# Message-passing network, two layers: where the transposes of the new rows lie in PSUM, and the order of the sums

## Chip, cores, metric

One core of a Trainium2 chip. The metric is the device time of one execution in microseconds, the median of the runs; lower is better. All times below are microseconds unless marked ns.

## What is computed

Two graph layers over 50,000 nodes of 160 values (64 scalars and 32 vectors of 3) and 50,000 edges sorted by `dst`. In both, a small network of the edge's features gives 192 weights for each edge, the source's row is multiplied by them and by the edge's four harmonics, the messages are summed by `dst`, and a linear map goes over the sums.

```python
h = jnp.maximum(_layernorm(x, axis=-1), 0.0)
x = x + _L0_gnn_ref(h, edge_attr_4, edge_attr_8, ...)        # layer 1
h = jnp.maximum(_layernorm(x, axis=-1), 0.0)
x = x + _L1_gnn_ref(h, node_vec1, src, dst, edge_attr_4, edge_attr_10, ...)   # layer 2

# in _L0_gnn_ref
xs, xv = s @ W1_s / np.sqrt(MUL0), jnp.einsum('nmc,mk->nkc', v, W1_v) / np.sqrt(MUL1)
w = jax.nn.silu(edge_embed @ fc_w1 + fc_b1) @ fc_w2 + fc_b2
msg = jnp.concatenate([m0_a, m0_b, m1_a..., m1_b...], axis=1)   # w * xs[src], xv[src] * sh
agg = jax.ops.segment_sum(msg, dst, num_segments=n) / np.sqrt(AVG_DEG)
out = agg @ W2 + node_features @ Wsc      # gates: silu(out_s), vectors times gates
return node_features + feats
```

## The kernel before

`one_layer` is called twice, with `first` true for layer 1. Everything that follows is about layer 1 unless it says otherwise. The work is cut into NB = 205 turns (41 steps of 5 pairs); a turn `t` has two tiles of 128 edges and two of 128 nodes. Each engine runs a `step` for s = 0, 1, ..., in which `T(k)` is the turn s-k: the stages of one turn are spread over nine steps. Within an engine the order of the stages is the order of the calls in `step`, written out by hand; between engines there are semaphores. `eng.wait_ge(sem, n)` holds the engine's queue until sem is n, `hold` does the same and leaves it out for counts of 0 or less. A stage adds 1 to its semaphore when its last instruction is done, so `wait_ge(xw_done, t.n + 1)` waits for the stage of turn t.n itself.

TensorE's step: sums of tile 0 of T(4) (L1607), radial product of T(2) (L1567), sums of tile 1 of T(4) (L1607), outputs of T(5) (L1622, L1629), `pre` of T(8) (L1651, the next layer's products of the new rows), edges of T(2) (L1583, L1586, L1590), `transposes2` of T(7) (L1639, the new rows after norm and relu, `h2`), `transposes` of T(1) (L1553, L1556).

ScalarE's step: feature casts for layer 2 in some turns (L544), `copy_hT2` of T(8) (L1475), `copy_hT` of T(2) (L1413), `copy_agg` of T(4) (L1449), the hidden activation of T(2) (L1395), `node_h2` of T(7) (L1466), `node_h` of T(1) (L1404, the `hn` pair), `scale_pre` of T(8) (L1483), `gates` of T(5) (L1458), the issue of the DMA that stores `base_tab` (L1511, behind a wait for `scale_pre`'s end), and `copy_xw` of T(2) (L1422 and, scaled by a harmonic, two of L1429), whose end is `scaled_ready`. The next radial product waits for it.

PSUM has eight banks of 512 float32 columns. Before, `front_ps` takes four: the transposes for `hT` fill columns 0 to 767 of its flattened width (bank 0 and half of bank 1), `hT2_ps` columns 768 to 1151 (the other half of bank 1 and the first 128 columns of bank 2), and `xw_ps` is banks 2 and 3, with the edges' products from column 128 of each and the radial product in the first 128 of bank 3. `agg_ps` and `out_ps` have two banks each; `agg_ps` holds 384 columns of each bank, one bank for each tile.

An engine may not read a bank while TensorE writes into it, so the code waits by bank. Bank 2 is shared by a third of `hT2_ps` and the products that `copy_xw` reads; hence two waits that the change takes out:

```python
hold(act, hT2_done, t.n - 4)                                            # copy_xw, t = T(2)
pe.wait_ge(scaled_ready, t.n + 1 if t.serial else min(t.n + 5, NB))     # transposes2, t = T(7)
```

With t = T(2) the first is for the transposes of T(7) of the same step.

After the loop a serial pass handles nodes with very many edges, then layer 2 runs with the same code and fewer stages.

Of the kernel before, what the change touches and what calls it, by code (L numbers as in the profile page):

```python
# [33 lines left out]
P = 128  # L34
# [7 lines left out]
NT = P  # L42
# [96 lines left out]
def build(nc, x, node_col, edge_rec, dst_rows, dst_next, row_last, dst_flat, ee, wts, out):  # L139
# [10 lines left out]
    with ExitStack() as ctx:  # L150
# [85 lines left out]
        front_ps = ps("front_ps", [P, 2 * PAIR, 512])  # L236
        agg_ps = ps("agg_ps", [P, PAIR, 512])
# [523 lines left out]
def one_layer(nc, ctx, layer, node_rows, edge_rows, new_dram, v):  # L761
# [9 lines left out]
    front_ps, agg_ps, out_ps = v["front_ps"], v["agg_ps"], v["out_ps"]  # L771
    hT_ps, xw_ps = front_ps[:, 0:PAIR, :], front_ps[:, PAIR:2 * PAIR, :]
    front = front_ps[:, :, :].rearrange("p b c -> p (b c)")
# [7 lines left out]
    both_ps, hT2_ps = front[:, 0:HE + HN], front[:, HE + HN:HE + 2 * HN]  # L781

    if first:
        hid_ps = xw_ps[:, 1, 0:P]
        w_ps = xw_ps[:, :, P:P + xw]
    else:
        hid_ps = xw_ps[:, 1, 0:PAIR * P].rearrange("p (j e) -> p j e", j=PAIR)
        w_ps = xw_ps[:, 0, 0:PAIR * WN].rearrange("p (j c) -> p j c", j=PAIR)
# [129 lines left out]
    with nc.Block() as block:  # L918
# [470 lines left out]
        def _(act):  # L1389
# [18 lines left out]
            def copy_hT(t):  # L1408
                b = t.tiles
                act.wait_ge(hT_done, t.n + 1)  # L1410
                hold(act, out_done, t.freed_m(RING))
                hold(act, xw_done, t.freed(RING))
                act.activation(hT[:, t.slot, :], both_ps, ACT.Relu).then_inc(hT_copied, 1)  # L1413

            def copy_xw(t):
                b = t.tiles
                act.wait_ge(xw_done, t.n + 1)
                hold(act, msg_ready, t.freed(2))
                if first:
                    if not t.serial:  # L1420
                        hold(act, hT2_done, t.n - 4)
                    act.copy(xw_sb[:, t.half, 0:b, 0:D + W_SS], w_ps[:, 0:b, 0:D + W_SS]).then_inc(xw_copied, 1)  # L1422
                    act.wait_ge(she_ready, t.n + 1)
                else:
                    act.copy(xw_sb[:, t.half, 0:b, D:D + W_SS], w_ps[:, 0:b, 0:W_SS]).then_inc(xw_copied, 1)
                    if t.serial:
                        act.wait_ge(win_in[t.slot], window_loads(t))
                for j in range(b):
                    ins = act.activation(xw_sb[:, t.half, j, D + W_SS:D + WN], w_ps[:, j, xw - SW:xw] if first else w_ps[:, j, W_SS:WN],  # L1429
                                         ACT.Copy, scale=harmonics(t)[:, j, 0:1])  # L1430
                ins.then_inc(scaled_ready, 1)
# [38 lines left out]
            def copy_hT2(t):  # L1470
                b = t.tiles
                act.wait_ge(hT2_done, t.m + 1)
                wait_hT(act, hT_done, t, PRE - 2)
                hold(act, pre_done, t.freed_m(1))
                act.copy(hT2[:, :], hT2_ps).then_inc(hT2_copied, 1)  # L1475
# [63 lines left out]
        def _(pe):  # L1539
# [9 lines left out]
            def transposes(t):  # L1549
                hold(pe, hT_copied, t.freed(1))  # L1550
                pe.wait_ge(he_ready, t.n + 1)
                for c in range(PARTS_X):
                    pe.transpose(front[:, c * P:(c + 1) * P], pair_cols(he[:, t.half, c, :, :]), ident[:, :])  # L1553
                pe.wait_ge(hn_ready, t.n + 1)
                for c in (2, 0, 1):
                    ins = pe.transpose(front[:, node_cols(c):node_cols(c) + NT], pair_cols(hn[0:NT, t.half, c, :, :]), ident[0:NT, 0:NT])  # L1556
# [38 lines left out]
            def sums(t, tiles):  # L1595

                flat = msg[:, :, :, :, :].rearrange("p h j c m -> p h j (c m)")
                if tiles[0] == 0:
# [10 lines left out]
                if tiles[-1] == t.tiles - 1:  # L1609
# [23 lines left out]
            def transposes2(t):  # L1633
# [3 lines left out]
                pe.wait_ge(scaled_ready, t.n + 1 if t.serial else min(t.n + 5, NB))  # L1637
                for c in range(PARTS_X):
                    ins = pe.transpose(hT2_ps[:, c * NT:(c + 1) * NT], pair_cols(h2[:, c, :, :]), ident[0:NT, 0:NT])  # L1639
# [17 lines left out]
            def step(T):  # L1657
                if t := T(4):
                    sums(t, [0] if first else [0, 1])
                if (t := T(2)) and first:  # L1660
                    radial(t)
                if (t := T(4)) and first:
                    sums(t, [1])
# [127 lines left out]
```

## Time and profile before

| | |
|---|---|
| median of 3 runs | 2412.83 (2403.69 to 2425.43) |
| the profiled execution, its own time | 2389.98 |
| its span, first to last instruction | 2388.2 |
| TensorE matmul busy | 2176.7 (91%) |
| TensorE weight loads busy | 2045.3 (86%) |
| VectorE busy | 1909.6 (80%) |
| ScalarE busy | 1930.8 (81%) |
| GpSimd busy | 1541.1 (65%) |
| mean granted TensorE clock | 0.968 of full |

The trace names instructions by the line of the kernel and groups them; `PEld` is a weight load of TensorE, `ACTq` an instruction of ScalarE's queue that issues a DMA. Busy shares are means over the whole program; layer 1's loop is the first three fifths of it. The ends of matmuls are modelled.

### The profile page before, as it was taken

To read this page: it belongs to the slowest core of one execution; us is meant where nothing else is said; L and a number is where in the kernel's file an instruction comes from. 1 tells how busy PE (TensorE), PEld (TensorE's weight loads), DVE (VectorE), ACT (ScalarE), POOL (GpSimd) and SP (SyncE) were. 2 spreads that over 40 slices of the span, in tenths; PEclk is the share of its full clock that TensorE was granted. 3 is DMA by queue.
4 is the path that set the end of the run, shared out by engine and by line. 5 is a ranking of instruction groups with operands and counts; after the bars stand their busy time and mean duration, and the time that the engine had idled before them with its cause. 6 is when DMAs were issued, how large, how long until landed. Compare 5 with 4: busy or idle time off the path is not lost. (4 is left out here: it accounts for less than half of the span.)

```text
span 2388.2 us, 79221 instructions
## 1 busy us (share of the span) xinstructions
PE 2176.7 (91%) x22003; PEld 2045.3 (86%) x22004; DVE 1909.6 (80%) x8636; ACT 1930.8 (81%) x5167; POOL 1541.1 (65%) x1925
## 2 busy tenths in 40 slices
PE   0889999999999999999999999559999999999997
PEld 0788888889999899899999999359999998999996
DVE  5878998789899898898889988227777777777775
ACT  2677898788888888798889988338888888888885
POOL 4766888778878887777777776145555554554550
PEclk9999999999999999999999999669999999999998
DMA  5456557644445545444444443247777776776772
GB/s 156 90 147 146 142 146 204 175 125 131 126 129 132 125 131 134 116 132 132 132 127 132 133 131 105 64 111 191 190 189 191 190 188 178 189 186 176 197 189 76
DMA packets 498819, 351.30 MB, mean 147 GB/s; under 512 B 188108, under 2 KB 484030, under 8 KB 498382
## 3 DMA queue, kind: packets, MB, share of 16 engines
q1 hardware_dynamic: 401007, 209.61, 34.3%
q0 software_dynamic: 41472, 69.42, 13.0%
q10 hardware_dynamic: 55904, 67.22, 8.1%
q8 instruction: 182, 2.98, 0.5%
q14 instruction: 254, 2.08, 0.3%
HBM read 199.00 MB, written 151.77 MB: 147 GB/s over the span
## 5 line engine op out<-in xcount | busy, mean ns | idle before, releaser
L1060 POOL DMA_INDIRECT xg<-table,from_row x411 | 397.9, 968 | 422.3 <-DVE msg L1233 229.1
L1622 PE MATMUL out_ps<-w_out,aggT 128*128 128x128 f32 (+1 forms) x4932 | 604.6, 273 | 17.4 <-issue 14.3
L1622 PEld LDWEIGHTS out_ps<-w_out,aggT 128*128 128x128 f32 x4932 | 591.6, 194 | 21.3 <-issue 19.4
L1060 POOL DMA_INDIRECT xg<-in_x,win x411 | 484.7, 1179 | 148.8 <-issue 127.5
L1607 PE MATMUL agg_ps<-sel,msg 128*128 128x128 f32 x3708 | 525.9, 284 | 27.5 <-issue 16.0
L1607 PEld LDWEIGHTS agg_ps<-sel,msg 128*128 128x128 f32 x3708 | 463.4, 195 | 37.0 <-issue 25.2
L1438 ACT ACTIVATE msg<-pw,win 128x64 f32<-128x64 f32 x1233 | 341.3, 352 | 5.2 <-issue 2.9
L1449 ACT COPY aggT<-agg_ps 128x768 f32<-128x768 f32 (+1 forms) x310 | 247.4, 798 | 96.0 <-PE agg_ps L1607 56.6
L1073 POOL TENSOR_TENSOR rs<-ve,neghalf 128x4 f32<-128x4 f32 x206 | 224.2, 1088 | 17.1
L1404 ACT ACTIVATE hn<-xn,nmr,rs 128x192 f32<-128x192 f32 x411 | 201.2, 540 | 41.5 <-DVE nmr L1165 41.2
L1483 ACT ACTIVATE kept<-out_ps,a_sb 128x320 f32<-128x320 f32 x410 | 193.9, 525 | 49.0 <-PE out_ps L1651 35.0
L1422 ACT COPY xw_sb<-front_ps 128x512 f32<-128x512 f32 x206 | 120.6, 586 | 112.4 <-PE front_ps L1639 91.1
L1082 POOL TENSOR_SCALAR ve<-mv 128x2 f32<-128x2 f32 x206 | 76.8, 373 | 205.3 <-DVE mv L1274 170.4
L1466 ACT ACTIVATE h<-kept,nmr,rs 128x192 f32<-128x192 f32 x411 | 201.7, 546 | 3.6 <-DVE nmr L1281 3.6
L1257 DVE SCALAR_TENSOR_TENSOR kept<-out_ps,a_sb,kept 128x160 f32<-128x160 f32 x410 | 138.4, 379 | 73.3 <-PE out_ps L1622 37.5
L1241 DVE TENSOR_TENSOR fe<-out_ps,fe 128x192 f32<-128x192 f32 x206 | 73.4, 356 | 150.4 <-ACT fe L1458 143.1
L1592 PE MATMUL front_ps<-w_fc,hid 100*128 100x192 f32 x822 | 182.2, 345 | 11.0 <-issue 10.0
L1651 PE MATMUL out_ps<-w_pre,hT 64*128 64x128 f32 (+1 forms) x2466 | 185.3, 281 | 5.8 <-ACT hT L1475 5.3
L1583 PE MATMUL front_ps<-w_lin,hT 64*128 64x64 f32 (+1 forms) x2466 | 174.9, 273 | 8.0 <-issue 3.8
L1629 PE MATMUL out_ps<-w_sc,hT 64*128 64x96 f32 (+2 forms) x2466 | 179.8, 278 | 0.0
L1084 POOL TENSOR_TENSOR rs<-ve,neghalf 128x2 f32<-128x2 f32 x206 | 168.1, 816 | 17.2
L1607 PE MATMUL front_ps<-sel,msg 128*128 128x128 f32 x1224 | 161.5, 282 | 17.1 <-issue 13.2
(194 smaller groups left out, 5039.2 us busy)
## 6 DMA issues: line engine op xcount, KB each, us to landing
base_tab<-kept ACTq DMA_DIRECT2D x205, 320.0 KB
kept<-base_tab SPq DMA_DIRECT2D x205, 320.0 KB
xn<-in_x SPq DMA_DIRECT2D x411, 80.5 KB, 1.8
table<-kept SPq DMA_DIRECT2D x410, 80.0 KB
out<-kept SPq DMA_DIRECT2D x410, 80.0 KB
ee_sb<-ee_parts SPq DMA_DIRECT2D x411, 22.5 KB, 1.8
ee_parts<-part SPq DMA_DIRECT2D x45, 196.0 KB
ee_sb<-ee_parts SPq DMA_DIRECT2D x411, 18.0 KB
```

Source lines behind the costliest of these rows:

```text
L1060: pool.indirect_dma_start(out=xg[:, t.slot, j, 0:D], out_offset=None, in_=edge_rows, in_offset=bass.IndirectOffsetOnAxis(ap=at, axis=0)).t ...
L1073: pool.tensor_tensor(rs[:, t.half, :, 0:b], ve[:, :, 0:b], neghalf[:, 0:2 * b].rearrange("p (a b) -> p a b", a=2), ALU.pow).then_inc(rs_re ...
L1404: ins = act.activation(hn[0:NT, t.half, :, j, :], in_parts(xn[0:NT, t.slot, j, :]), ACT.Relu, bias=nmr[0:NT, t.half, j:j + 1], scale=rs[0: ...
L1438: ins = act.activation(msg[:, t.half, j, 1 + c, 0:MUL0], pw[:, j, :], ACT.Copy, scale=harmonics(t)[:, j, 1 + c:2 + c])
L1449: act.copy(aggT[:, t.half, 0:b, :, :], sums_ps[t.half][:, 0:b, 0:BLOCKS * NT].rearrange("p j (k n) -> p j k n", k=BLOCKS)).then_inc(aggT_c ...
L1466: ins = act.activation(h2[:, :, j, :], in_parts(kept[:, t.slot, j, 2 * D:]), ACT.Relu, bias=nmr2[:, t.half, j:j + 1], scale=rs2[:, t.half, ...
L1483: act.activation(kept[:, t.slot, j, 0:2 * D].rearrange("p (k c) -> p k c", k=2), pre_ps[0:NT, j, :, :], ACT.Copy, scale=node_attr(t, j)).t ...
L1592: ins = pe.matmul(w_ps[:, j, :], hid[0:hidden, t.half, j, :], w["fc2_"][:, :], start=True, stop=True)
L1607: ins = pe.matmul(sums_ps[t.half][:, j, k * NT:(k + 1) * NT], flat[:, t.half, j, k * P:(k + 1) * P], sel[:, t.half, j, :], start=not t.ser ...
L1622: ins = pe.matmul(rows[0:NT, j, c0:c1], aggT[:, t.half, j, k, :], w[f"out{k}_"][:, :], start=fresh, stop=True, skip_group_check=not fresh)
L1629: ins = pe.matmul(rows[0:NT, j, c0:c1], hT[r, t.slot, n0:n0 + NT], w["sc"][r, c0:c1], start=False, stop=True, skip_group_check=True)
L1651: ins = pe.matmul(pre_ps[0:NT, j, :, c0:c1], hT2[r, c * NT:(c + 1) * NT], pre_w[r, 2 * c0:2 * c1].rearrange("p (k c) -> p k c", k=2), star ...
```

## The change

`near_ps` has four banks: 0 and 1 for `hT` (384 columns of each), 2 and 3 are `agg_ps`. `hT2_ps` lies in columns 384 to 511 of banks 0, 1 and 2. `xw_ps` gets two banks of its own. `copy_xw` no longer waits for the transposes of the new rows, and these no longer wait for `scaled_ready`, but for the sums' copy of T(4). The sums of tile 0, which write bank 2, wait for `copy_hT2` of T(8) of the same step; they change places with the sums of tile 1. All other hunks follow from the new addresses.

```diff
-        front_ps = ps("front_ps", [P, 2 * PAIR, 512])
-        agg_ps = ps("agg_ps", [P, PAIR, 512])
+        near_ps = ps("near_ps", [P, 2 * PAIR, 512])
+        agg_ps = near_ps[:, PAIR:2 * PAIR, :]
+        xw_ps = ps("xw_ps", [P, PAIR, 512])
         out_ps = ps("out_ps", [P, PAIR, 512])
...
-    both_ps, hT2_ps = front[:, 0:HE + HN], front[:, HE + HN:HE + 2 * HN]
+    both_ps, hT2_ps = near_ps[:, 0:PAIR, 0:HE], near_ps[:, 0:PARTS_X, HE:HE + NT]
...
-                act.activation(hT[:, t.slot, :], both_ps, ACT.Relu).then_inc(hT_copied, 1)
+                act.activation(hT[:, t.slot, :].rearrange("p (k c) -> p k c", k=2), both_ps, ACT.Relu).then_inc(hT_copied, 1)
...
                 if first:
-                    if not t.serial:
-                        hold(act, hT2_done, t.n - 4)
                     act.copy(xw_sb[:, t.half, 0:b, 0:D + W_SS], w_ps[:, 0:b, 0:D + W_SS]).then_inc(xw_copied, 1)
...
-                act.copy(hT2[:, :], hT2_ps).then_inc(hT2_copied, 1)
+                act.copy(hT2[:, :].rearrange("p (c n) -> p c n", c=PARTS_X), hT2_ps).then_inc(hT2_copied, 1)
...
             def sums(t, tiles):
 
                 flat = msg[:, :, :, :, :].rearrange("p h j c m -> p h j (c m)")
-                if tiles[0] == 0:
+                if first and not t.serial and 0 in tiles:
+                    hold(pe, hT2_copied, t.n - 3)
+                if len(tiles) == 2 or tiles[0] == (1 if first and not t.serial else 0):
                     pe.wait_ge(msg_ready, t.n + 1)
...
-                if tiles[-1] == t.tiles - 1:
+                if len(tiles) == 2 or tiles[0] == 0:
                     ins.then_inc(agg_done, 1)
...
                 wait_hT(pe, hT_copied, t, PRE - 3)
-                pe.wait_ge(scaled_ready, t.n + 1 if t.serial else min(t.n + 5, NB))
+                if not t.serial:
+                    pe.wait_ge(aggT_copied, min(t.n + 4, NB))
                 for c in range(PARTS_X):
-                    ins = pe.transpose(hT2_ps[:, c * NT:(c + 1) * NT], pair_cols(h2[:, c, :, :]), ident[0:NT, 0:NT])
+                    ins = pe.transpose(hT2_ps[:, c, :], pair_cols(h2[:, c, :, :]), ident[0:NT, 0:NT])
...
                 if t := T(4):
-                    sums(t, [0] if first else [0, 1])
+                    sums(t, [1] if first else [0, 1])
                 if (t := T(2)) and first:
                     radial(t)
                 if (t := T(4)) and first:
-                    sums(t, [1])
+                    sums(t, [0])
```

## Rows read from the trace of the kernel before

**Rows 1.** Busy time of each engine (count) in layer 1's loop, clock, DMA share, GB/s.

```profile
62.04:1467.21 1405.17, 1350.55 (x15265) 1255.88 (x15266) 1230.19 (x6056) 1203.35 (x2789) 1095.52 (x1440) 0.98 0.52 135
```

**Rows 2.** Who waited for whom, 60 to 1467: total, times, longest.

```profile
ACT xw_sb L1422 <- PE front_ps L1639: 88.8, 172, 2.5
PEld front_ps L1567 <- issue: 63.9, 193, 2.1
```

**Rows 3.** ScalarE in order of time, one turn: start, length, instruction, idle before.

```profile
1018.62 0.59 ACT L1422 COPY xw_sb<-front_ps 128x512 f32<-128x512 f32 x1 [0.47 <-PE front_ps L1639]
1019.11 0.58 ACT L1429 ACTIVATE xw_sb<-front_ps,she 128x96 f32<-128x96 f32 x2
1019.57 0.49 ACT L1475 COPY hT<-front_ps 128x384 f32<-128x384 f32 x1
1019.92 0.84 ACT L1413 ACTIVATE hT<-front_ps 128x768 f32<-128x768 f32 x1
1020.86 0.80 ACT L1449 COPY aggT<-agg_ps 128x768 f32<-128x768 f32 x1
...
1022.60 0.98 ACT L1404 ACTIVATE hn<-xn,nmr,rs 128x192 f32<-128x192 f32 x2
1023.64 0.95 ACT L1483 ACTIVATE kept<-out_ps,a_sb 128x320 f32<-128x320 f32 x2
1024.48 0.33 ACT L1458 ACTIVATE fe<-out_ps 128x192 f32<-128x192 f32 x1
1024.62 0.52 ACTq L1511 DMA_DIRECT2D base_tab<-kept  x1
1025.27 0.59 ACT L1422 COPY xw_sb<-front_ps 128x512 f32<-128x512 f32 x1 [0.46 <-PE front_ps L1639]
```

**Rows 4.** TensorE's weight loads in order of time, the same turn.

```profile
1018.88 0.75 PEld L1607 LDWEIGHTS agg_ps<-sel,msg 128*128 128x128 f32 x6
1019.80 0.13 PEld L1567 LDWEIGHTS front_ps<-ee_sb,fc_parts 75*128 75x128 bf16 x2 [0.17 <-issue]
1019.89 0.75 PEld L1607 LDWEIGHTS agg_ps<-sel,msg 128*128 128x128 f32 x6
1020.55 1.42 PEld L1622 LDWEIGHTS out_ps<-w_out,aggT 128*128 128x128 f32 x12
```

**Rows 5.** TensorE's matmuls in order of time, the same turn.

```profile
1022.73 0.86 PE L1651 MATMUL out_ps<-w_pre,hT 64*128 64x128 f32 x12
...
1024.61 0.55 PE L1639 MATMUL front_ps<-ident,h 128*128 128x128 f32 x3
```

**Rows 6.** All engines in order of time, another turn's end.

```profile
1011.07 0.55 PE L1639 MATMUL front_ps<-ident,h 128*128 128x128 f32 x3
...
1011.31 0.54 ACTq L1511 DMA_DIRECT2D base_tab<-kept  x1
...
1011.97 0.59 ACT L1422 COPY xw_sb<-front_ps 128x512 f32<-128x512 f32 x1 [0.47 <-PE front_ps L1639]
```

**Rows 7.** All engines in order of time, the end of a turn near 473.

```profile
471.47 0.52 ACTq L1511 DMA_DIRECT2D base_tab<-kept  x1
...
472.46 0.90 PE L1639 MATMUL front_ps<-ident,h 128*128 128x128 f32 x3
...
473.47 0.59 ACT L1422 COPY xw_sb<-front_ps 128x512 f32<-128x512 f32 x1 [1.81 <-PE front_ps L1639]
```

**Rows 8.** All records of L1511: shortest, median, longest in ns, first and last start.

```profile
L1511 ACTq DMA_DIRECT2D base_tab<-kept x205: 520/538/636, 104.3 to 1520.0; - x103
```

**Rows 9.** ScalarE in order of time, near 353 and near 643.

```profile
353.17 2.34 ACT L544 CAST part<-found_i 128x784 bf16<-128x784 f32 x3
355.40 0.50 ACT L1475 COPY hT<-front_ps 128x384 f32<-128x384 f32 x1
...
356.47 0.83 ACT L1449 COPY aggT<-agg_ps 128x768 f32<-128x768 f32 x1
...
643.61 0.80 ACT L1449 COPY aggT<-agg_ps 128x768 f32<-128x768 f32 x1 [0.60 <-PE agg_ps L1607]
```

More of the change, by code:

```diff
@@ L770, in one_layer @@
     st2, mv2, ve2, rs2, nmr2, h2, hT2 = (v[k] for k in ("st2", "mv2", "ve2", "rs2", "nmr2", "h2", "hT2"))
-    front_ps, agg_ps, out_ps = v["front_ps"], v["agg_ps"], v["out_ps"]
-    hT_ps, xw_ps = front_ps[:, 0:PAIR, :], front_ps[:, PAIR:2 * PAIR, :]
-    front = front_ps[:, :, :].rearrange("p b c -> p (b c)")
+    near_ps, agg_ps, xw_ps, out_ps = v["near_ps"], v["agg_ps"], v["xw_ps"], v["out_ps"]
+    hT_ps = near_ps[:, 0:PAIR, :]
     a_sb, long_a, node_col = v["a_sb"], v["long_a"], v["node_col"]
@@ L785, in one_layer @@
         w_ps = xw_ps[:, :, P:P + xw]
+        assert HE == HN == BLOCKS * NT
     else:
@@ L1552, in transposes @@
                 for c in range(PARTS_X):
-                    pe.transpose(front[:, c * P:(c + 1) * P], pair_cols(he[:, t.half, c, :, :]), ident[:, :])
+                    pe.transpose(hT_ps[:, 0, c * P:(c + 1) * P], pair_cols(he[:, t.half, c, :, :]), ident[:, :])
                 pe.wait_ge(hn_ready, t.n + 1)
                 for c in (2, 0, 1):
-                    ins = pe.transpose(front[:, node_cols(c):node_cols(c) + NT], pair_cols(hn[0:NT, t.half, c, :, :]), ident[0:NT, 0:NT])
+                    ins = pe.transpose(hT_ps[:, 1, node_cols(c) - HE:node_cols(c) - HE + NT], pair_cols(hn[0:NT, t.half, c, :, :]), ident[0:NT, 0:NT])
                 ins.then_inc(hT_done, 1)
```

## The prediction

> **What bounds the kernel now.** I first read the busy times by stretch. The first layer's loop, from its first to its last record of the x·W copy (L1422), takes 1405 us for 204 intervals, 6.89 us a turn; TensorE is busy for 96% of it, ScalarE for 86%, VectorE for 88% [rows 1]. A share of 96% looks like an engine that waits for nobody, but the ends of matmuls are modelled, so the second view is who waits for whom. It has TensorE idle at the weight load of the radial product (L1567) 193 times, 63.9 us in all, and ScalarE idle ahead of L1422 172 times, 88.8 us, put down to the transposes of the new rows (L1639) [rows 2]. That second row is the wait that the change takes away, so the question is whether L1639 truly ends it. A row of waits names the last releaser by semaphore; it doesn't see an instruction that holds the engine's own queue.
>
> The third view is the order of time in one turn. 116 of the 200 intervals between successive L1422 records are 6.64 to 6.67 us long; one stands in the rows, 1018.62 to 1025.27. Its loop can be followed without a gap. The L1422 copy starts at 1018.62, the scaled copies behind it (L1429) end at 1019.69 [rows 3]. TensorE, whose sums of tile 0 were issued from 1018.88, starts the radial product's weights 0.11 later, at 1019.80, then sums of tile 1 at 1019.89, and the output products at 1020.55 [rows 4]. The `pre` products end at 1023.59 [rows 5]; ScalarE starts on them (L1483) 0.05 later, 1023.64. Its L1483 pair ends at 1024.59, and at 1024.62 ScalarE's queue begins to issue the store of `base_tab` (L1511), until 1025.14. The next L1422 starts 0.13 behind that [rows 3]. So the loop is TensorE from radial to `pre`, then ScalarE from L1483 over the DMA issue to L1429, then TensorE again. Both engines have a little slack inside it, and the loop has none.
>
> **Which of two things holds L1422.** In that turn the transposes end at 1025.16 [rows 5], 0.11 before L1422, and the DMA issue 0.13 before it: a tie. Two other turns break it. At 1011.97 L1422 starts 0.35 behind the transposes' end (1011.62), with TensorE's records at their usual spacing, and again 0.12 behind the end of the DMA issue [rows 6]. At 473.47, with TensorE late, it starts 0.11 behind the transposes (473.36) and 1.48 behind the DMA issue [rows 7]. So each of the two can hold the copy, and what follows either is 0.11 to 0.13. The issue's own length doesn't stretch with the waiting behind it: 520 to 636 ns over all 205 [rows 8], 0.52 in the turn where the copy came 1.5 us later [rows 7]. It is a cost of its own, and stays.
>
> **The change, part by part.**
> *The wait for the transposes ahead of L1422 goes.* What is late next is the DMA issue, at the same place to 0.02 us. Gain 0.00 to 0.01 a turn. The wait instruction itself goes too: what lies between the issue's end and the copy is 0.13, with three waits in it, against 0.11 from a semaphore to the radial weights with none left. The bounds are 0 and 0.04; I take 0, since the two rows hardly differ.
>
> *A wait for the copy of the transposed rows comes ahead of the sums of tile 0.* The last 128 columns of `agg_ps` bank 0 now hold a third of `hT2_ps`; `sums` waits for `hT2_copied` at t.n-3, with t the turn's T(4). In turn s that is s-7 copies, thus the copy of T(8), L1475 of this very turn. On ScalarE that is the first thing behind L1429: it runs from 1019.57 to 1020.06 [rows 3]. Its release reaches a weight load 0.11 later, as L1429's does: 1020.17. Today the second group of sums starts at 1019.89 [rows 4], and the change puts tile 0 in that place. So it starts 0.28 later. Sums of tile 1 move to the front, where they take the same 0.66 as tile 0 did, and need bank 1 alone; they don't shorten this, since the radial product waits for L1429 either way and fills 0.09 of what is left. What is queued behind the new wait on TensorE is everything to the turn's end: sums, outputs, `pre`, the edges' products, both groups of transposes. From the sums' first weight load to the next L1422 it is 5.38 (1019.89 to 1025.27), without a gap to absorb anything. The turn becomes 1.55 + 5.38 = 6.93 where it is 6.65. ScalarE gives nothing back: its sums copy L1449 moves from 1020.86 to 1021.14, then 1.74 to the first `hn` (1022.60 less 1020.86) and 0.88 for the pair where nothing holds it bring it to 1023.76, and `pre` releases L1483 at 1023.92, still later.
>
> *The transposes' own waits.* The wait for `scaled_ready` at t.n+5 goes; the edges' products, ahead of them in the queue, wait for the same count, so nothing is gained. The new one wants the sums' copy of T(4). L1449 ends at 1021.66 [rows 3], 1021.94 when shifted; the transposes come at 1024.61 [rows 5], 1024.89 shifted. The cover is 2.9 us, and without it TensorE's transposes and the next sums would be late by what is missing.
>
> *Layout.* Transposes write three banks in place of two, `hT_ps` gets a gap of 128 columns in each bank, and the copies read runs of 384 and 128. Today's copy of 768 columns in one run takes 0.84 and that of 768 in two runs of 384 takes 0.80 [rows 3]. For L1475 with three runs no row stands; between -0.02 and +0.02 by those, and I take 0. Layer 2 and the serial pass get other bank addresses and the same waits, at no cost: nothing there runs beside these columns.
>
> *How many turns pay.* There are 205 turns; the first 8 have no copy to wait for. In 25 of the 195 turns whose records are whole, L1483 follows the `hn` pair by 0.88 in place of 1.04: ScalarE itself sets it, after a delay of its own such as that at 643.61, where L1449 comes 0.60 late [rows 9]; such a gap hides up to all of the 0.28. 205 - 8 - 25 is 172. In eight turns casts for layer 2's features sit ahead of L1475, 2.34 us of them at 353.17 [rows 9]. There L1449 comes 1.07 behind L1475's start (356.47 less 355.40). It will come 0.49 for L1475 itself, 0.11 for its release and 0.97 for the sums (1019.89 to 1020.86) behind it, 1.57 in all: 0.5 more, or some 0.25 above the 0.28. Sum: 172 x 0.28 = 48, and 8 x 0.25 = 2, thus +50 us. On the profiled execution's own 2390 us that makes 2440. That execution ran 23 us below the median of the three runs, 2412.8; carried over to it, **2463 us**.
>
> **The rivals.**
> *Rival A, the copy does come forward (faster).* If the DMA issue doesn't hold the copies behind it, L1422 starts once the gates are done, near 1024.81 [rows 3], 0.46 earlier; the edges' products that it reads are out by then, since the transposes behind them start at 1024.61 [rows 5]. The turn is 6.93 - 0.46 = 6.47, above TensorE's floor of 6.65 less its stall of 0.26 ahead of the radial product. 0.18 x 197 turns is 35 us less: 2378. For it speak the waits' row, 88.8 us [rows 2], and the tie; against it rows 6, where TensorE had long been done and the copy still came with the issue's end. The Trainium skill ("DMA: Bandwidth & Descriptors", "Anatomy of one DMA — SWDGE (gpsimd) path") gives some 50 ns for a sequencer's dispatch of a DMA. By that the copy would come forward nearly all the way, and the sum would be rival A's; the row of 520 to 636 ns is was taken on this very queue, and I hold to it. Chance 0.13.
>
> *Rival B, the two cancel.* Were the queue held for only part of the issue, so that the copy moves up by g, a turn is worth 0.28 - g. At g = 0.28 the change turns from a loss to a gain, and g from 0.2 to 0.36 leaves it within 16 us of 2413, under the 24 us that are 1% (about what a measurement of this kernel can tell from no change). The same result comes where the serial delays of ScalarE in the slower 84 of 200 intervals hide the wait far more often than I counted. Chance 0.11.
>
> *The forecast itself* says that the change doesn't do what it says: the wait removed wasn't the one that held. Chance 0.76.
>
> **The range.** Within the forecast, the turns that pay are between 150 and 197, at 0.24 to 0.30: 36 to 59 us, with 2 to 5 for the casts, thus 2451 to 2477. The three runs of before lie from 2404 to 2425, 12 us to either side, so 2440 to 2489. With rival B taken in down to 2402 the range is 2402 to 2489, and leaves out rival A. Slower by over 1% (above 2437): 0.76. Within 1%: 0.11. Faster: 0.13.
>
> **What the profile after would show.** If I am right: L1422 still 0.12 to 0.13 behind the end of L1511, and now well behind the edges' products, with its idle time as long as before and another releaser's name; TensorE idle some 0.3 between the radial product and the sums of tile 0, put down to L1475; L1449 0.28 later after L1422; turns of 6.93. If rival A is right, L1422 starts ahead of the end of L1511, or L1511's record is short, and the turns are near 6.47. What would make me wrong: an L1475 released or finished earlier than its row shows, or a DMA issue that was long only because a full queue behind it kept it so.

## The result, and the profile after

The changed kernel takes 2518.04 us (median of 4 runs, 2509.12 to 2524.09) against 2416.91 (2403.69 to 2425.43, 4 runs) of the kernel before on the same chip: ratio 1.0428 [1.0384, 1.0472], 101 us slower. 2463 us were forecast, in a range up to 2489. Ratios, with their 95% intervals, are worked out from the single runs, leaving out one of run 10 that was slow (2521.46), and so differ a little from the quotient of two medians. The profiled execution's span is 2518.2 us at a granted clock of 0.954.

The loop of layer 1, from the first to the last copy of x·W (now L1421), by stretch; columns as in [rows 1]:

```profile
60.86:1609.77 1548.91, 1439.68 (x15573) 1311.50 (x15574) 1249.91 (x6151) 1220.16 (x2843) 1062.67 (x1457) 0.97 0.47 124
```

It is 7.59 us for each of 204 intervals. Over the same stretch of before, from 62.04 to 1493.85, it was 7.02. It holds the same 15573 matmuls, 6151 instructions of VectorE and 2843 of ScalarE there; so no work was added. ScalarE's busy time is even 6 us shorter, and on ScalarE all of the 117 us that the loop grew by in these two executions is waiting. TensorE's busy time, by modelled ends, is 62 us longer for the same matmuls; of that the clock, 0.97 against 0.98, makes some 14 us at most, and the runs don't explain the rest.

Who waited for whom, 60 to 1610 us, of after (total, times, longest):

```profile
ACT aggT L1448 <- PE near_ps L1608: 106.4, 151, 3.9
PEld xw_ps L1566 <- issue: 90.2, 109, 2.7
ACT xw_sb L1421 <- issue: 85.6, 188, 0.9
ACT aggT L1448 <- remote: 51.0, 22, 2.8
PEld near_ps L1608 <- ACT hT L1474: 38.2, 146, 2.4
```

Three readings. The wait of [rows 2] that the change took away has only changed its name: ScalarE still stands ahead of the x·W copy, 85.6 us in 188 places where it was 88.8 in 172, put down to "issue" instead of to the transposes. (The 88.8 end at 1467; over the whole loop all idle time ahead of that copy is 110.0 before and 109.7 after.) The new wait, the sums behind the copy of the transposed rows (L1474), costs 38.2 us in 146 places, 0.26 each. And there is a row that I had not foreseen: ScalarE waits for the sums themselves ahead of their copy (L1448).

Two turns of after, ScalarE, TensorE and GpSimd in order of time, show where that comes from; only the lines that bear on it are shown. The first is undisturbed:

```profile
1017.18 0.54 ACTq L1510 DMA_DIRECT2D base_tab<-kept  x1
1017.81 0.59 ACT L1421 COPY xw_sb<-xw_ps 128x512 f32<-128x512 f32 x1 [0.45 <-issue]
1018.75 0.49 ACT L1474 COPY hT<-near_ps 128x384 f32<-128x384 f32 x1
1018.80 0.96 POOL L1061 DMA_INDIRECT xg<-in_x,win  x1 [0.31 <-issue]
1018.99 0.13 PEld L1566 LDWEIGHTS xw_ps<-ee_sb,fc_parts 75*128 75x128 bf16 x2 [0.82 <-issue]
1019.30 0.94 PE L1608 MATMUL near_ps<-sel,msg 128*128 128x128 f32 x6
1020.07 1.45 PE L1623 MATMUL out_ps<-w_out,aggT 128*128 128x128 f32 x12
1020.37 0.80 ACT L1448 COPY aggT<-near_ps 128x768 f32<-128x768 f32 x1 [0.41 <-PE near_ps L1608]
...
1024.03 0.52 ACTq L1510 DMA_DIRECT2D base_tab<-kept  x1
1024.65 0.59 ACT L1421 COPY xw_sb<-xw_ps 128x512 f32<-128x512 f32 x1 [0.43 <-issue]
...
1025.59 0.49 ACT L1474 COPY hT<-near_ps 128x384 f32<-128x384 f32 x1
1026.13 0.94 PE L1608 MATMUL near_ps<-sel,msg 128*128 128x128 f32 x6
1026.42 1.04 POOL L1061 DMA_INDIRECT xg<-in_x,win  x1 [0.31 <-issue]
1026.90 1.45 PE L1623 MATMUL out_ps<-w_out,aggT 128*128 128x128 f32 x12
1027.90 0.80 ACT L1448 COPY aggT<-near_ps 128x768 f32<-128x768 f32 x1 [1.11 <-PE near_ps L1608]
1029.65 0.98 ACT L1405 ACTIVATE hn<-xn,nmr,rs 128x192 f32<-128x192 f32 x2
1030.53 0.93 ACT L1482 ACTIVATE kept<-out_ps,a_sb 128x320 f32<-128x320 f32 x2
1032.12 0.59 ACT L1421 COPY xw_sb<-xw_ps 128x512 f32<-128x512 f32 x1 [0.45 <-issue]
```

In the first turn the x·W copy comes 0.09 and 0.10 behind the end of the DMA issue. The sums' second group starts 0.31 behind the radial weights (0.09 in [rows 4]), 0.06 behind the end of L1474. The turn is 6.84. In the second the sums' products end at 1027.07, and their copy, which needs nothing else, starts at 1027.90: 0.83 behind. It then sets everything after it on ScalarE, up to the `pre` pair (L1482), which waits for the second `hn` activation and not for its products. The turn is 7.47.

A count over all turns of the trace, of where a copy of the sums starts 0.3 to 3 us behind the modelled end of its last product, gives 79 of 203 after, with 93 us in sum, and 24 of 203 before, with 28 us. In all 79 ScalarE stands idle meanwhile. In 7 of the 24 it doesn't: they lie beside the casts, and their copy queues behind other work of ScalarE. 89 turns of after are under 6.9 us, where 144 of before were.

The trace also has the times at which the semaphores change. In 76 of the 79 late turns the change that the copy waits for stands in it, 0.38 to 2.5 us (median 0.86) behind the modelled end of the last product, and the copy starts 0.02 behind the change in each of them; in undisturbed turns the change comes 0.01 behind that end. TensorE itself isn't late: in all 79 its next products (L1623) start 0.16 ahead of the modelled end of the sums, as they do in undisturbed turns. So neither ScalarE nor the order of work on TensorE makes the delay; it lies between the time at which the last product should be out and the change of its semaphore.

What lies beside the late copy is the second of GpSimd's two gathers of a turn: the sums end 0.65 behind its start (1027.07 and 1026.42). In before, sums and gather in the turn of [rows 3]:

```profile
1019.94 0.89 PE L1607 MATMUL agg_ps<-sel,msg 128*128 128x128 f32 x6
1020.80 0.96 POOL L1060 DMA_INDIRECT xg<-in_x,win  x1 [0.31 <-issue]
1020.86 0.80 ACT L1449 COPY aggT<-agg_ps 128x768 f32<-128x768 f32 x1
```

The sums end at 1020.83, just as the gather begins, and the copy is on time. So ended 78 of the 203 turns of before, within 0.3 behind the start of the second gather, and 4 of them were late. After has 48 turns that end 0.3 to 0.9 behind it, and 41 of them are late; before had 15 of that kind, 4 of them late. The first gather does the same: 26 turns of after end 0.3 to 1.0 ahead of the second gather's start, beside the first, and 18 of them are late. Counted from the start of whichever gather came last, the sums end 0.2 to 0.8 behind it in 94 turns of after, 69 of them late, and 1.6 or more behind it in 56, 2 of them late.

### The profile page after: what moved, and what is told of

It is laid out like the page before. It is cut to its first block and busy times, and to the rows that moved or that the text cites. A ratio compares the mean times of both kernels' runs of the same rounds, so it can differ in the third digit from the quotient of the medians.

```text
span 2518.2 us, 79220 instructions
## 1 busy us (share of the span) xinstructions
PE 2247.2 (89%) x22003; PEld 2083.1 (83%) x22004; DVE 1909.1 (76%) x8636; ACT 1924.2 (76%) x5167; POOL 1496.2 (59%) x1925
## 5 line engine op out<-in xcount | busy, mean ns | idle before, releaser
L1608 PE MATMUL near_ps<-sel,msg 128*128 128x128 f32 x4932 | 705.0, 287 | 62.6 <-issue 30.7
L1608 PEld LDWEIGHTS near_ps<-sel,msg 128*128 128x128 f32 x4932 | 616.0, 196 | 113.0 <-issue 57.8
L1623 PE MATMUL out_ps<-w_out,aggT 128*128 128x128 f32 (+1 forms) x4932 | 610.5, 275 | 14.1 <-issue 10.0
L1623 PEld LDWEIGHTS out_ps<-w_out,aggT 128*128 128x128 f32 x4932 | 597.8, 196 | 17.6 <-issue 14.6
L1061 POOL DMA_INDIRECT xg<-in_x,win x411 | 449.0, 1093 | 148.6 <-issue 129.1
L1448 ACT COPY aggT<-near_ps 128x768 f32<-128x768 f32 x412 | 328.8, 798 | 272.9 <-PE near_ps L1608 187.2
L1405 ACT ACTIVATE hn<-xn,nmr,rs 128x192 f32<-128x192 f32 x411 | 201.0, 539 | 39.8 <-DVE nmr L1166 38.2
L1074 POOL TENSOR_TENSOR rs<-ve,neghalf 128x4 f32<-128x4 f32 x206 | 217.3, 1055 | 17.2
L1482 ACT ACTIVATE kept<-out_ps,a_sb 128x320 f32<-128x320 f32 x410 | 192.6, 521 | 42.6 <-PE out_ps L1653 33.2
L1421 ACT COPY xw_sb<-xw_ps 128x512 f32<-128x512 f32 x206 | 120.7, 586 | 112.1 <-issue 85.6
L1591 PE MATMUL xw_ps<-w_fc,hid 100*128 100x192 f32 x822 | 183.0, 346 | 14.1 <-issue 11.9
L1582 PE MATMUL xw_ps<-w_lin,hT 64*128 64x64 f32 (+1 forms) x2466 | 176.6, 276 | 11.7 <-issue 7.8
L1582 PEld LDWEIGHTS xw_ps<-w_lin,hT 64*128 64x128 f32 x2466 | 164.0, 196 | 14.5 <-issue 12.2
```

The costliest lines, as they stand in the source:

```text
L1061: pool.indirect_dma_start(out=xg[:, t.slot, j, 0:D], out_offset=None, in_=edge_rows, in_offset=bass.IndirectOffsetOnAxis(ap=at, axis=0)).t ...
L1074: pool.tensor_tensor(rs[:, t.half, :, 0:b], ve[:, :, 0:b], neghalf[:, 0:2 * b].rearrange("p (a b) -> p a b", a=2), ALU.pow).then_inc(rs_re ...
L1405: ins = act.activation(hn[0:NT, t.half, :, j, :], in_parts(xn[0:NT, t.slot, j, :]), ACT.Relu, bias=nmr[0:NT, t.half, j:j + 1], scale=rs[0: ...
L1448: act.copy(aggT[:, t.half, 0:b, :, :], sums_ps[t.half][:, 0:b, 0:BLOCKS * NT].rearrange("p j (k n) -> p j k n", k=BLOCKS)).then_inc(aggT_c ...
L1482: act.activation(kept[:, t.slot, j, 0:2 * D].rearrange("p (k c) -> p k c", k=2), pre_ps[0:NT, j, :, :], ACT.Copy, scale=node_attr(t, j)).t ...
L1582: pe.matmul(lin_ps[:, j, c0:c1], hT[r, t.slot, c * P:(c + 1) * P], w["lin"][r, c0:c1], start=True, stop=True)
```

## The experiments

They ran in four jobs, each on another chip: runs 1 to 4, then 5, 6, 8 and 9, then 7 and 10 to 12, then 13. The kernel before took 2405, 2305, 2404 and 2308 us there (medians), so each ratio is to its own job's. I call the sums' copy "late" where it starts over 0.3 us behind the last product. The expectations of runs 5, 6, 8 and 9 name times for a chip where the kernel before takes 2400 us; theirs took 2305, so that only their ratios and turns can be held against them.

**1. The wait alone.** The kernel before, its order and layout unchanged, and the new wait ahead of the second group of sums:

```diff
             def sums(t, tiles):
...
+                if first and not t.serial and tiles == [1]:
+                    hold(pe, hT2_copied, t.n - 3)
```

> The kernel before, with one wait more: TensorE's second group of sums in a turn waits for the copy of the transposed new rows (copy_hT2) of the same step, as the changed kernel's does. Layout, order of the sums and all other waits stay as before. Theory 1 (the wait does it all: it puts the sums 0.20 us later, 205 times or 41 us, and the signal of their last matmul then falls where GpSimd issues the gathers, which costs some 60 us more): 2500 to 2530, and ScalarE's copy of the sums starts 0.8 us behind the last sum in about half the turns. Theory 2 (the new layout is what costs more than the wait: TensorE writes bank 2 while ScalarE reads banks 0 and 1): 2445 to 2460, and the copy starts 0.03 behind the sums as before.

2510.12 us (2505.46 to 2516.1), ratio 1.0431 [1.0391, 1.0471]. As expected by theory 1, that is the whole loss of the change. All that moves is this wait; the other order of the tiles, the layout of three banks and the transposes' own waits cost and give nothing that can be seen, each ratio being known to 0.4%. All idle time of ScalarE ahead of the copy of the sums, grouped by line, in this kernel, with what ended it:

```profile
L1449 ACT COPY aggT<-agg_ps 128x768 f32<-128x768 f32 x203 | 162.2, 799 | 157.8 <-PE agg_ps L1609 104.1 <-remote 40.9 <-issue 12.8
```

The same view of before and then of after:

```profile
L1449 ACT COPY aggT<-agg_ps 128x768 f32<-128x768 f32 x203 | 162.4, 800 | 44.2 <-PE agg_ps L1607 18.3 <-remote 8.2 <-issue 1.7
```

```profile
L1448 ACT COPY aggT<-near_ps 128x768 f32<-128x768 f32 x203 | 162.3, 799 | 169.9 <-PE near_ps L1608 106.4 <-remote 51.0 <-issue 12.5
```

**2. Neither wait.** The changed kernel with the third transpose written over the second in bank 1, so that bank 0 is free for the sums. It computes layer 2's products of the new rows with a third of them replaced.

```diff
-    both_ps, hT2_ps = near_ps[:, 0:PAIR, 0:HE], near_ps[:, 0:PARTS_X, HE:HE + NT]
+    both_ps, hT2_ps = near_ps[:, 0:PAIR, 0:HE], near_ps[:, 0:PAIR, HE:HE + NT]
...
-                act.copy(hT2[:, :].rearrange("p (c n) -> p c n", c=PARTS_X), hT2_ps).then_inc(hT2_copied, 1)
+                act.copy(hT2[:, :].rearrange("p (c n) -> p c n", c=PARTS_X), hT2_ps[:, 1:2, :].to_broadcast([P, PARTS_X, NT])).then_inc(hT2_copied, 1)
...
-                if first and not t.serial and 0 in tiles:
-                    hold(pe, hT2_copied, t.n - 3)
...
-                    ins = pe.transpose(hT2_ps[:, c, :], pair_cols(h2[:, c, :, :]), ident[0:NT, 0:NT])
+                    ins = pe.transpose(hT2_ps[:, min(c, 1), :], pair_cols(h2[:, c, :, :]), ident[0:NT, 0:NT])
```

> The changed kernel without the sharing of a sums bank: the third transpose of the new rows is written over the second (bank 1), the copy reads bank 1 three times, and the sums of tile 0 no longer wait for the copy. So a third of the transposed rows is wrong, with all instructions and sizes kept; ScalarE's copy_xw waits for no transposes here. It measures what the removed wait alone is worth. Theory of the prediction (the DMA issue on ScalarE's queue holds copy_xw at the same place): within 10 us of before, 2405 to 2425, with turns of 6.62 to 6.65 us and copy_xw 0.10 us behind the end of the DMA issue. Rival A (the copy comes forward 0.46 us): 2330 to 2380 and turns of 6.4. Theory 2 (layout costs): 2460 or more.

2404.11 us (2396.39 to 2419.97), ratio 1.0011 [0.9981, 1.0041]. The removed wait alone is worth nothing that the time shows. Its turn, ScalarE in order of time:

```profile
1017.17 0.58 ACT L1421 COPY xw_sb<-xw_ps 128x512 f32<-128x512 f32 x1 [0.45 <-issue]
...
1023.17 0.54 ACTq L1510 DMA_DIRECT2D base_tab<-kept  x1
1023.81 0.59 ACT L1421 COPY xw_sb<-xw_ps 128x512 f32<-128x512 f32 x1 [0.45 <-issue]
```

6.64 us, with the copy 0.10 behind the DMA issue's end: 0.02 to 0.03 less than in [rows 3], no more.

**3 and 4. Plain loads for gathers.** To take away what lies beside the late copies, the gathers of neighbour rows in layer 1 were replaced, in the changed kernel and in the one before, by loads of as many consecutive rows issued from SyncE. Both compute layer 1 from other neighbours' features.

```diff
+                        hold(sp, he_ready, t.freed(RING))
+                        for j in range(PAIR):
+                            sp.dma_start(xg[:, t.slot, j, 0:D], edge_rows[bass.ds(node_of(t, j), P), 0:D]).then_inc(xn_in[t.slot], 16)
...
             def gather(t):
+                if first and not t.serial:
+                    return
```

> The changed kernel with the same edit (wrong source rows, plain loads from SyncE's queue in place of GpSimd's gathers in layer 1's loop). Theory 1 (wait 0.20 a turn, the rest by signals held while the gathers are issued): all turns near 6.85, no late start of the copy of the sums, and 35 to 50 us above the same edit on the kernel before. Theory 2 (the loss beyond the wait has another cause than the gathers): 90 to 110 us above it, turns alternating between 6.85 and 7.5 as now.

> The kernel before with the two gathers by source row of each turn of layer 1 replaced by two plain loads of 128 consecutive rows, issued from SyncE's queue with the node rows; GpSimd issues no DMA in this loop. So the source rows are the wrong ones, with all sizes kept. The base for the run with the same edit on the changed kernel. Theory 1: TensorE's signals are no longer held, so turns are 6.65 with fewer long ones, and the time falls to 2340 to 2400. Theory 2: no such effect, 2400 to 2430.

Changed kernel 2463.62 us (2461.14 to 2473.17), ratio 1.025 [1.0209, 1.029]; kernel before 2442.18 (2437.84 to 2446.63), 1.0154 [1.0116, 1.0191]. No copy of the sums is late in layer 1 of the first, and in the second 6 are, all with ScalarE busy; the two differ by 21 us where they differed by 101. Theory 1 had 35 to 50 between them, and 2340 to 2400 for the kernel before: it came out slower than unedited. The loads brought stalls of their own, up to 19.6 us long (GpSimd behind VectorE's statistics, 694.1 and 766.5 us in all), which may hide part of any other delay. The lateness goes with the gathers; its price couldn't be read here.

Layer 2 of the same two executions is a control on the same chip, since its gathers were kept: there 154 and 147 of the 208 copies of the sums are late.

**5 and 6. The store of `base_tab` from SyncE,** in the changed kernel and in the one before. This takes the DMA issue off ScalarE's queue.

```diff
+                if first:
+                    sp.dma_start(base_tab[t.n], kept[:, t.slot, :, D:KEPT]).then_inc(stored[t.slot], 16)
...
-                    act.wait_ge(ev_ready, t.m * PAIR + PAIR)
-                    act.dma_start(base_tab[t.n], kept[:, t.slot, :, D:KEPT]).then_inc(stored[t.slot], 16)
```

> The changed kernel with the store of base_tab issued from SyncE's queue, with the store of the new rows one step later, in place of ScalarE's. It takes away what now holds copy_xw. Theory of the prediction (the DMA issue of 0.54 us on ScalarE's queue holds the copy at that place): copy_xw comes 0.4 us or more forward, right behind the gates and the edges' products, undisturbed turns go from 6.85 to 6.4 to 6.5, and the time falls by 60 to 90 us against the changed kernel, 2430 to 2460. Rival (the copy is held by something else): no change, 2500 to 2530.

> The kernel before with the same edit. Here copy_xw waits for the transposes of the new rows too, which end at the same place as the DMA issue does, so that nothing may come forward. Theory of the prediction (a tie of two causes): 2395 to 2415, turns of 6.62 to 6.65. If the wait for the transposes were not a cause at all: turns of 6.4, 2350 to 2370.

Changed kernel 2336.57 us (2330.58 to 2338.3), ratio 1.0124 [1.0097, 1.0151]; before 2342.54 (2329.93 to 2356.24), 1.0136 [1.0097, 1.0175]. With the issue gone, the wait for the transposes does hold the copy in the kernel before, as ScalarE and TensorE in order of time show:

```profile
1020.86 0.52 PE L1591 MATMUL front_ps<-w_fc,hid 64*128 64x192 f32 x4
...
1021.31 0.55 PE L1640 MATMUL front_ps<-ident,h 128*128 128x128 f32 x3
...
1021.97 0.59 ACT L1424 COPY xw_sb<-front_ps 128x512 f32<-128x512 f32 x1 [0.46 <-PE front_ps L1640]
```

In the changed one it follows the edges' products at once:

```profile
1024.56 0.52 PE L1590 MATMUL xw_ps<-w_fc,hid 64*128 64x192 f32 x4
...
1025.13 0.59 ACT L1423 COPY xw_sb<-xw_ps 128x512 f32<-128x512 f32 x1
```

The median turn is 6.53 against 6.65. So the change's gain exists in the turns, and the DMA issue is what covered it; in the time the two can't be told apart, as their intervals overlap. The new wait gives most of it back even here (run 7, without it, has turns of 6.11). What the expectations priced did not come: against the unedited changed kernel, 1.0148 in run 13, moving the store saves about 5 us and not 60 to 90. The store is worth more on ScalarE than on SyncE: moving it costs the kernel before 1.4%. VectorE then waits for the store of the new rows, which now stands behind it in SyncE's queue, 73.6 us in 46 places; in the trace of the kernel before, on another chip, it was 22.3 in 15.

**8 and 9. The gathers apart.** The second gather of a turn was put behind `rstd2`, the block of normalisation that GpSimd runs next in its step (the expectation of run 11 calls it the second block), in the changed kernel and in the one before; what it gathers is the same.

```diff
-                    gather(t)
+                    gather(t, [0] if first else None)
...
+                if (t := T(-1)) and first:
+                    gather(t, [1])
```

> The changed kernel with the two gathers of a turn no longer issued back to back on GpSimd: the second comes behind rstd2 in layer 1's step, some 3 us later. Everything else, the wait ahead of the sums of tile 0 too, stays. Theory 1 (TensorE's signals are held from about the second gather's issue to 0.5 us behind its end, and the added wait moved the sums into that time): the copy of the sums no longer starts late in half the turns, most turns are near 6.85, and the time falls to 2430 to 2480, unless the later gather now holds another signal. Theory 3 (signals are held by any gather, at whatever place, and only plain loads avoid it): no change against the changed kernel, 2500 to 2530.

> The kernel before with the same edit: the second gather of a turn behind rstd2 on GpSimd. The base for the run above, and a test of whether the long turns of the kernel before come from the same cause. Theory 1: 20 to 60 us faster, 2350 to 2390. Theory 3: 2400 to 2420. If the later gather holds up the statistics on GpSimd instead (it stands ahead of rstd): above 2430 with VectorE waiting for rs.

Changed kernel 2380.6 us (2375.26 to 2390.43), ratio 1.0334 [1.0303, 1.0365]; before 2374.56 (2371.98 to 2379.5), 1.0297 [1.0272, 1.0323]. This told nothing of the lateness: on this chip, where the kernel before takes 2305 us, no copy of the sums or of the `pre` products started over 0.3 late with ScalarE idle in any of the four kernels, with the gathers back to back (runs 5 and 6) or apart. (6 copies of the sums in run 6 and 7 in run 9 are that late with ScalarE at other work, mostly beside the casts.) It told two other things. Lateness belongs to some chips only. And moving the gather costs the kernel before 3% by itself: as the last case of run 9's expectation has it, VectorE waits for GpSimd's statistics (`rs`), 157.1 us in 163 places.

**10 to 12 and 7, a third chip.** Run 10 is the changed kernel unedited, 11 and 12 are the edits of 8 and 9 again, 7 is the edit of 2 with that of 5.

> The changed kernel, unedited, beside the others of this job. Two theories of its loss: (1) 0.20 us a turn that the sums start later (some 35 us in all) plus some 60 us from completion signals of TensorE that arrive late when a stage ends beside the second gather of the turn; (2) the wait for the copy of the sums is long in the changed kernel for a reason of its own, whatever the chip's signals do. On the chip where the kernel before took 2305 us no copy behind a TensorE stage started late. If this job falls on such a chip, (1) expects the ratio to fall from 1.042 to 1.012 to 1.02 and the copy of the sums 0.03 to 0.05 behind the last product in nine turns of ten; (2) expects 1.04. If it falls on one where the kernel before takes 2400 us and such copies are late, both expect 1.04 again, and the comparison with the gathers moved apart decides.

> The changed kernel with the second gather of a turn behind the second block of GpSimd's work. On a chip with late signals: if signals are late because a stage ends while two gathers are issued back to back, they are late at neither gather now, and the copy of the sums starts 0.03 to 0.05 behind their end; ratio about that of the other chip, 1.03. If a single gather's issue does it, lateness moves to the stages that end beside the moved gather, and the ratio is 1.04 to 1.06. On a chip without late signals: 1.03, as before.

> The same edit on the kernel before. On a chip with late signals: if the pair of gathers is what delays them, ratio 1.01 to 1.03 and the changed kernel with the same edit only 0 to 0.015 above it; if any gather does, the ratio is 1.03 to 1.05 with late stages at both gathers. On a chip without: 1.03, as before.

> Neither wait and no DMA issue on ScalarE's queue: the store of base_tab from SyncE, the third transpose over the second (the output is wrong in one third of the products of layer 2's new rows), no hold ahead of the sums. With the store moved, the kernel before had turns of 6.65 and the changed one turns of 6.53. If the edge copy is held by the transposes' wait and by the DMA issue, whichever comes last, and by nothing else, both gone give the whole 0.4 to 0.46 less the sums' added 0.2 back: turns of 6.3 to 6.4, and a ratio to the kernel before 0.01 to 0.03 under that of the changed kernel with the same store, 0.98 to 1.005. If instead some other step holds the turn at 6.5, the turns stay there and the time is that of the changed kernel with the store moved, 1.01.

This chip makes copies late. Changed kernel: 2506.12 us (2481.29 to 2521.46), ratio 1.0404 [1.0354, 1.0454]. With the gathers apart: 2464.73 (2464.07 to 2474.16), 1.0264 [1.0222, 1.0306]. Kernel before with the gathers apart: 2467.19 (2443.72 to 2472.99), 1.0229 [1.0176, 1.0281]. The edit that costs the kernel before 2 to 3% makes the changed kernel 41 us faster here. The copy of the sums in run 11, by line, and the turn that shows why, ScalarE and GpSimd in order of time:

```profile
L1451 ACT COPY aggT<-near_ps 128x768 f32<-128x768 f32 x205 | 163.8, 799 | 74.6 <-PE near_ps L1611 68.2 <-issue 6.4
```

```profile
1021.32 1.07 POOL L1062 DMA_INDIRECT xg<-in_x,win  x1 [0.20 <-issue]
...
1023.29 1.21 POOL L1075 TENSOR_TENSOR rs<-ve,neghalf 128x4 f32<-128x4 f32 x1
...
1023.74 0.80 ACT L1451 COPY aggT<-near_ps 128x768 f32<-128x768 f32 x1 [0.31 <-PE near_ps L1611]
1024.69 1.09 POOL L1062 DMA_INDIRECT xg<-in_x,win  x1 [0.20 <-issue]
```

One copy of the sums in 203 is late, where run 10 has 81 in 203, all 81 among the 152 turns where the sums end from 0.3 ahead of a gather's start to 1.6 behind it. The lateness went along with the gather. In run 12 it is the `pre` pair that starts over 0.3 behind its products, in 70 turns of 204: 67 of the 169 whose products end so close to a gather, and 3 of the other 35. In 60 of the 70 ScalarE is idle meanwhile. Run 9, the same kernel on the other kind of chip, has 30 such pairs, and ScalarE is busy in all 30. One of the mild ones:

```profile
794.47 1.10 POOL L1061 DMA_INDIRECT xg<-in_x,win  x1 [0.20 <-issue]
...
794.74 0.86 PE L1654 MATMUL out_ps<-w_pre,hT 64*128 64x128 f32 x12
...
795.93 0.94 ACT L1486 ACTIVATE kept<-out_ps,a_sb 128x320 f32<-128x320 f32 x2 [0.35 <-PE out_ps L1654]
```

So a single gather does it; it needn't be two in a row. That was the second of the two theories in these expectations. The times don't bear it out: it had 1.04 to 1.06 for run 11 and 1.03 to 1.05 for run 12, and both came out where the first had put them. The count of late pairs decides it, and the price that it set on them was too high.

Run 7 took 2419.93 us (2411.25 to 2440.49), ratio 1.008 [1.0046, 1.0115], above the 0.98 to 1.005 expected. Its turns are 6.11 at the limit of the shortest tenth, under the 6.3 expected, and 6.67 in the median, with 42 late copies. That late copies and the price of the moved store take what the shorter chain gives is the likely reading; it wasn't tested apart. No version among these beats the kernel before.

**13. The changed kernel on a chip without late copies.** Unedited.

> The changed kernel, unedited, once more, for a chip on which no copy behind a TensorE stage starts late (where the kernel before takes some 2305 us). There the sums' 0.20 us a turn is all that the change can cost: ratio 1.010 to 1.020, turns of 6.85 in nine of ten that are not stalled, the copy of the sums 0.03 to 0.05 behind the last product. If the ratio there is 1.04, the late copies are not what costs 60 us, and that part of the theory falls. On a chip with late copies: 1.04, and nothing new.

It fell on such a chip. 2340.78 us (2336.59 to 2346.4) against 2307.6 (2302.75 to 2317.22), ratio 1.0148 [1.0121, 1.0175], 33 us. The sums' copy by line (5 of the 208 stand behind layer 1's loop):

```profile
L1448 ACT COPY aggT<-near_ps 128x768 f32<-128x768 f32 x208 | 166.2, 799 | 79.8 <-PE near_ps L1608 73.2 <-issue 6.5
```

and a turn in order of time, with the sums' end 0.65 behind the start of the second gather, as in the late turn of after:

```profile
1025.73 0.94 PE L1608 MATMUL near_ps<-sel,msg 128*128 128x128 f32 x6
1026.02 1.16 POOL L1061 DMA_INDIRECT xg<-in_x,win  x1 [0.30 <-issue]
1026.51 1.45 PE L1623 MATMUL out_ps<-w_out,aggT 128*128 128x128 f32 x12
1026.70 0.80 ACT L1448 COPY aggT<-near_ps 128x768 f32<-128x768 f32 x1 [0.31 <-issue]
```

The copy starts 0.03 behind the products' end (1026.67). No copy of the sums is late in 204 turns, and 165 turns are under 6.9.

**Layer 2, in all traces.** Its stages are the same in every run, but for addresses in PSUM. From the last copy of x·W of layer 1's loop to the program's end it takes 820 to 826 us in the five traces from chips without lateness, with 1 of 208 copies of the sums late, and 894 to 925 in the other ten, with 142 to 156 late.

## Why the prediction was wrong

Its direction held, and so did what it said of the wait taken out. The price of the new wait did not: 50 us forecast for it, 101 measured. Two errors are in that, of opposite sign. The wait itself costs less than forecast, 33 us on a chip without late copies, and something that the forecast didn't have costs the rest.

- *The removed wait is worth nothing.* Right, at 0.02 to 0.03 us a turn (bounds 0 to 0.04, taken as 0). Run 2 shows it by itself, runs 5 and 6 show that the DMA issue is what covers it. Rival A falls with it. The Trainium skill's 50 ns for a sequencer's dispatch of a DMA ("DMA: Bandwidth & Descriptors", "Anatomy of one DMA — SWDGE (gpsimd) path") is given for a DMA that GpSimd issues, and the prediction set it against one that ScalarE issues. On ScalarE's queue the issue lasts 0.52 to 0.54 us in the rows shown here, and the copy starts 0.09 to 0.13 behind it.
- *The new wait costs 0.28 a turn.* Too much by a quarter. I let the release of L1474 reach TensorE after 0.11; it takes 0.06. That gives 0.22, less the 0.02 to 0.03 above: turns of 6.84 where I had 6.93.
- *172 turns pay.* About right: 33 us on the chip of run 13 are 0.20 in 165 turns.
- *Turns with casts.* Right: in run 13 the sums' copy comes 1.52 behind the start of L1474 where the casts end at 358.30 (358.30 and 359.82); I had 1.57.
- *Layout and the transposes' waits cost nothing.* Right, by run 1 against the change.
- *204 intervals in 1405 us, 6.89 a turn.* Misread: 1467.21 is the 201st copy of x·W, the loop's last is at 1493.85, and the mean turn is 7.02. No term of the sum hangs on it.
- *"From the sums' first weight load to the next L1422 it is 5.38 (1019.89 to 1025.27), without a gap to absorb anything."* This is the step that failed. I shifted the whole rest of the turn by a constant, as though what follows a TensorE stage followed it at the same distance wherever it lands. In the undisturbed turn of after it is 5.35 (1019.30 to 1024.65), in the late one 5.99 (1026.13 to 1032.12). On the chips of the first result and of runs 1 to 4 and 7, 10 to 12, a copy that waits for a stage which ends beside a GpSimd gather starts 0.3 to 2.5 us late. In the kernel before, the sums ended ahead of the second gather or as it began in 152 turns of 203; 0.2 later many end inside it. 62 more copies that are late with ScalarE idle, 79 against 17, and some 75 us more in sum, with nearly no slack behind them, stand beside the 68 us that the change costs on such a chip above its 33 elsewhere. Run 13, on another chip, had no lateness with the kernel unchanged; run 11 lost it by moving the gather, with the wait unchanged. The idle time ahead of that copy is 75 to 80 us in these two, and 163 to 170 in run 10 and after.

The kernel before held the clue: 17 of its own copies of the sums were late with ScalarE idle. I took the one at 643.61 [rows 9], with its 0.60 of waiting, for a delay of ScalarE that would hide the new wait, and didn't look at what was next to it: a gather that had started at 643.00, with the sums ending at 643.07. The forecast's own range ended at 2489 because it had no case in which a later stage meets something.

What stays open is what inside the chip delays the change of the semaphore. That a gather beside the end of the stage is the condition, on such a chip, is shown by runs 3, 11 and 12, and by layer 2 of runs 3 and 4; that the delay lies neither in ScalarE nor in TensorE's order of work, by the times of the semaphores and of TensorE's next products. Nor do the runs say why two of the four jobs' chips don't do it. Of the 100 us between these chips in the kernel before, some 70 stand in layer 2, where three copies of the sums in four are late on the one kind and one in 208 on the other.

## What to carry to other kernels

Before counting a removed wait as a gain, find what else stands on that engine's queue at the same place; here a DMA issue of half a microsecond made the wait free. A wait added to a chain without slack costs its shift in every turn, and then whatever the shifted stages collide with: lay the other engines' records beside the place where each stage will end, not only where it starts. Where a profile of before has the same instruction late in one turn of ten, find out beside what, before moving it there in all of them.

## What the hardware showed unexpectedly

- On the two chips where the kernel before takes 2404 us, and on that of the first result (2417), the semaphore of a TensorE stage often changes up to a microsecond late, and sometimes 2, when the stage ends beside the issue of a GpSimd gather (79 of 203 copies of the sums over 0.3 us late, 1.2 in the mean; the copy starts 0.02 behind the change, and TensorE's next products are on time). On the two chips where it takes 2305 to 2308 us no such delay is in the traces, with the same program and the same gathers (0 of 204).
- The same edit had another sign from chip to chip: the gathers apart bring the changed kernel from 1.0404 to 1.0264 on one, while on another it stands at 1.0334, above the 1.0148 that the unedited one has on a third chip, of that second kind.
- TensorE's sums started 0.06 us behind the end of the ScalarE copy that they wait for, where the radial weights start 0.11 behind theirs [rows 3, 4].
